# A four-layer graph network on one core: another order of VectorE's round in the second edge layer

## The reference

```python
h = jnp.maximum(_layernorm(x, axis=-1), 0.0)
e = jnp.concatenate([h[src], h[dst]], axis=-1)
e = jax.nn.relu(e @ Wm1 + bm1) @ Wm2 + bm2
e = e * drop_mask                                  # edge_attr_96
m = jax.ops.segment_sum(e, dst, num_segments=n)
z = jnp.concatenate([h, m], axis=-1)
x = x + jax.nn.relu(z @ Wu1 + bu1) @ Wu2 + bu2
```

## Time and profile before

| what | value |
|---|---|
| time, middle of three runs | 6119.12 us (6116.01 to 6123.38) |
| the profiled execution's own time | 6117.6 us |
| its span, from first to last instruction | 6115.7 us |
| busy: PE, DVE, ACT, POOL | 75%, 69%, 57%, 56% of the span |
| the pass `e1` | some 2480 to 3395 us from the span's start |

### The profile page before, as it was taken

The page is one execution under the profiler, slowest core; times in us unless marked ns, Lnnn a source line. Parts: engine busy times, 40 slices in busy tenths (PEclk is TensorE's granted clock), DMA queues, the critical chain, the costliest instruction groups (busy, mean ns, idle before and its releaser), DMA issues. The chain is left out here.

```text
span 6115.7 us, 115642 instructions
## 1 busy us (share of the span) xinstructions
PE 4559.9 (75%) x22351; PEld 2931.6 (48%) x22351; DVE 4229.4 (69%) x13899; ACT 3505.4 (57%) x8824; POOL 3410.0 (56%) x3543
## 2 busy tenths in 40 slices
PE   5776888888799999799999788878888984222222
PEld 1223555555444444466666566656656663222221
DVE  5667888888788888777777688878876663222222
ACT  6996666666699999555555455545545552111110
POOL 0004666666654443344343566566657776777777
PEclk9999999999999999899999787778778885555555
DMA  0002333333344443455555577656657773222222
GB/s 18 0 0 67 101 105 102 104 103 105 98 96 94 94 94 86 105 143 142 141 142 137 150 188 193 181 148 163 163 144 183 184 187 89 61 64 66 63 67 57
DMA packets 1144861, 677.32 MB, mean 111 GB/s; under 512 B 898421, under 2 KB 1096833, under 8 KB 1144744
## 3 DMA queue, kind: packets, MB, share of 16 engines
q1 hardware_dynamic: 1031784, 527.07, 31.7%
q0 software_dynamic: 112960, 148.99, 11.7%
HBM read 445.59 MB, written 232.61 MB: 111 GB/s over the span
## 5 line engine op out<-in xcount | busy, mean ns | idle before, releaser
L724 POOL DMA_INDIRECT xs<-t,idx x1176 | 1110.5, 944 | 951.5 <-DMA idx<-at 573.4
L1197 PE MATMUL bank<-ident,msg 128*96 128x128 f32 (+1 forms) x1568 | 305.5, 329 | 856.5 <-ACT msg L992 771.8
L724 POOL DMA_INDIRECT xs<-c,idx x784 | 763.9, 974 | 291.6 <-issue 233.2
L992 ACT ACTIVATE msg<-xs,now 128x96 f32<-128x96 f32 x784 | 229.3, 364 | 1071.4 <-DMA xs<-c,idx 715.3
L1041 PE MATMUL bank<-cols,before 128*128 128x384 f32 x1756 | 734.0, 520 | 17.3 <-DVE wu_out L1334 14.1
L1495 DVE TENSOR_TENSOR_SCAN aggT<-goes,aggT,bank 96x512 f32<-96x512 f16 (+1 forms) x490 | 620.7, 1267 | 133.9 <-PE bank L1150 115.0
L1197 PEld LDWEIGHTS bank<-ident,msg 128*96 128x96 f32 (+1 forms) x1568 | 218.6, 163 | 1022.7 <-ACT msg L992 650.1
L1208 PE MATMUL bank<-w,aggT 96*128 96x96 f32 (+1 forms) x3136 | 549.9, 334 | 105.2 <-DVE aggT L1495 104.6
L1670 DVE SCALAR_TENSOR_TENSOR y<-bank,now,rows 128x96 f32<-128x96 f32 x392 | 97.2, 310 | 719.1 <-PE bank L1208 719.1
L724 POOL DMA_INDIRECT xd<-in_x_dram,idx x392 | 373.9, 954 | 395.5 <-DVE xn L1565 228.6
L1208 PEld LDWEIGHTS bank<-w,aggT 96*128 96x128 f32 (+1 forms) x3136 | 517.3, 249 | 130.9 <-issue 88.6
(11 more groups left out here) (233 smaller groups left out, 10943.2 us busy)
## 6 DMA issues: line engine op xcount, KB each, us to landing
t<-xn SPq DMA_DIRECT2D x294, 192.0 KB, 2.2
xd<-t SPq DMA_DIRECT2D x294, 192.0 KB, 3.5
goes<-goes_d SPq DMA_DIRECT2D x392, 128.0 KB
xd<-in_x_dram SPq DMA_DIRECT2D x196, 192.0 KB
t<-xo SPq DMA_DIRECT2D x196, 192.0 KB
hd<-t SPq DMA_DIRECT2D x196, 192.0 KB
hs<-t SPq DMA_DIRECT2D x196, 192.0 KB
c<-xn SPq DMA_DIRECT2D x196, 192.0 KB
```

The source lines that it names most:

```text
L724: nc.gpsimd.indirect_dma_start(out=into, out_offset=None, in_=table, in_offset=bass.IndirectOffsetOnAxis(ap=indices, axis=0)).then_inc(don ...
L1197: ins = nc.tensor.transpose(bank[g.at(2)][0:m, c * P:(c + 1) * P], msg[:, g.at(2), c, 0:m], ident[:])
```

## The change

VectorE's list for `e1` is put in another order; no instruction is added or taken away, and no wait is changed.

```diff
                 else:
                     sums = sums_of(ph, lambda g: bank[5][0:D, :], ph["seg"], D, ph["z"])
-                    stages = [(spread, 2), (times_drop, 3), (home_x, 2), (new_x, 5), (edge_moments, 0), (of_round, 0), (sums, 3)]
+                    stages = [(edge_moments, 0), (of_round, 0), (spread, 2), (times_drop, 3), (home_x, 2), (new_x, 5), (sums, 3)]
                 pipelined(dve, EG, stages)
```

## The result

The changed kernel takes 6168.52 us (middle of four runs, 6161.38 to 6173.45), the kernel before 6120.66 (middle of four runs as well): a ratio of 1.0079, 95% interval 1.0063 to 1.0095. It is slower, by 48 us; forecast were 32 us, and a time of 6150 in a range from 6117 to 6172. The profiled execution took 6168.8 us, 51.2 more than the one before.

A forecast was written before the change was run, and what follows sets the result against it. The prediction took PE, waiting on ACT in a 9.02 us ring, to bound the pass; a new VectorE-PE ring of 9.40 us in the loop, 9.29 outside, would add 32 us, giving 6150 us, range 6117 to 6172.

The forecast's parts named there:

- the ring of PE and ACT without VectorE: PE's L1114 waits for ACT's normalizing of `hd`, released by `home_z`; claimed to bind before the change, 9.02 us a round.
- Earlier roots gain nothing: Roots come a round earlier for ACT; claimed no gain, since ACT's normalizing stood idle 0.0 us before `hd`.
- The moments' inputs keep their lead: POOL's gathers ahead of VectorE's moments; claimed the lead shrinks to 23 us and stays, at no cost.
- The new ring: L1150, `sums`, moments, roots, `spread`, `times_drop`, then PE's L1126, L1128, L1150; claimed to bind at 9.40 us in the loop, chance 0.79.
- PE's wait at L1126: PE's `hid` product should wait for `times_drop` in nearly every round, some 0.1 to 0.4 us.
- The sum: All steps from one `sums` to the next: 9.40 us in the loop, 9.29 outside, 875.4 us in 93 rounds.
- last step to `spread`: VectorE's gap from the roots' last operation to `spread`: 0.26 us in the loop, 0.15 in written-out rounds.
- The 0.16 us more between `spread` and `times_drop` in each of 14 turns: Extra VectorE time between these two operations at each turn of the loop, 2.2 us in all.
- the 9.3 to 9.5 that were named as a sign: Round time in us of pass `e1` expected in the changed profile if the forecast held.
- the cover just holds: Rival: `times_drop` still comes in time for L1126, so the time stays at 6119 us; chance 0.13.
- the kernel gets faster: Rival: PE's wait for ACT at L1114 shrinks, by 0.55 us a round at most, down to 6067 us; chance 0.04.
- The clock: Rival: new PE waits make TensorE's clock fall in the pass, giving 6171 to 6290 us; chance 0.04.

The follow-up runs named there:

- e7: Kernel before, with ACT running `home_act` between its two normalizing halves and PE `home_u` between its two transpose halves; 6051.0 us, ratio 0.9897.
- e1: Changed kernel with `sums` put back behind the roots, so only moments and roots work a group further ahead; 6115.2 us, ratio 0.9999 to the kernel before.
- e3: Changed kernel with `times_drop` run before `spread`; 6115.6 us, ratio 1.0001 to the kernel before.
- e5: Changed kernel with one more VectorE operation each round, between the roots and `spread`; 6181.3 us, ratio 1.0107 to the kernel before.
- e6: Changed kernel with one more VectorE operation each round, between `new_x` and `sums`; 6161.5 us, ratio 1.0076 to the kernel before.
- e8: Changed kernel with ACT running `home_act` between its normalizing halves and PE `home_u` between its transpose halves; 6168.3 us, ratio 1.0087 to the kernel before.
- e4: Changed kernel with `spread`'s three waits and turn count moved ahead of the moments; 6138.7 us, ratio 1.0036 to the kernel before.
- e2: Kernel before with `sums` moved in front of moments and roots, which do not work a group further ahead; 6695.0 us, single run.
- e10: Changed kernel with only `spread`'s turn count moved ahead of the moments, its three waits left in place; 6153.2 us, single run.
- e9: Changed kernel with `spread`'s turn count and waits moved ahead of the moments, except the flags' wait; 6151.6 us, single run.

## Why the prediction was right, point by point

- **What bounds the pass before**: the ring of PE and ACT without VectorE. Shown by e7, where cutting it takes 63 us out. It gives more than the 0.55 us a round that PE stood idle, 0.63. Idle time counts from the recorded end of the product before, and in the kernel before four transposes (L1150) are recorded with 0.60 us where the next product starts 0.43 us after them; an idle time of 0.55 can so stand for up to 0.72, which would cover the 0.08. That this is the reason was not tested.
- **Earlier roots gain nothing**: shown by e1. The rule of the Trainium skill that was named there (Perfetto Trace Analysis, "Optimization Strategies": when the matmul engine idles for others, optimize those that block it) agrees with the runs where it is applied to what PE waits for: e7 reorders ACT's list and gains; e1 brings ACT an input that it did not lack, and does not. The row that the prediction read for this, of `hd` in the earlier trace rows, could not show a wait for roots, since ACT waits for them in front of `hs`. The row of `hs` in the kernel before, in the same window, reads 0.0 as well, so the conclusion held:

```profile
L825 ACT ACTIVATE hs<-xs,nmr,rstd 128x96 f32<-128x96 f32 x376 | 143.8, 456 | 0.0
```

- **The moments' inputs keep their lead**: shown by e1. POOL waits longer for `home_x`, 142.0 us in 21 waits (2520 to 3420 us) where it was 3.4 in 11, which the forecast did not say; but VectorE never waits for a gather in that window, so the lead hides it.
- **The new ring and PE's wait at L1126**: shown by e3 (taken off, the loss is gone), e5 against e6 (an operation costs on it and not beside it) and e8 (the other ring does not matter).
- **The sum** was too small by 18.7 us (875.4 forecast, 894.1 measured from `sums` of group 1 to that of group 94). The step that failed is "last step to `spread`": 0.26 us was taken, for one computed address, and the loop's rounds show 0.44. That is 0.18 x 84 = 15 us of the 18.7, and one more comes from the written-out rounds, where 0.15 was taken and the later ones show 0.23. Of the rest, moments and roots took 3.56 us on average where 3.51 was taken, 4.6 us more, and `times_drop` 0.53 where 0.56 was taken, 3.0 us less. The 0.16 us more between `spread` and `times_drop` in each of 14 turns did not come: that pair is 1.20 us apart in every round, where 1.17 was taken, and the two misses cancel by luck. The three waits and the count that stand in front of `spread`, with the register operations that belong to them, were not counted; e4 shows that they make 0.33 of the 0.44. The upper bound of the step, 0.61, held, and so did the range, in which the time lies near the upper end. The round, 9.61 us, lies above the 9.3 to 9.5 that were named as a sign, and near the 9.7 that was to mean a mis-sized term, which it did.
- **The rivals.** That the cover just holds fell with the measured ratio, that the kernel gets faster with it and with e1. The clock did not fall in the changed kernel: 1.00 in the window, with two stalls of PE in each round. It fell in e2, where PE waits 3.15 us in one piece. The rule of the Trainium skill (TensorE: Matmul & The Clock Gate, "A second HAM failure mode: psum-queue depth-cycling"), that short idles between groups of matmuls make the clock swing, does not agree with the changed kernel, whose stalls of 0.30 and 0.55 us left the clock at 1.00. The clock of e2 does fall (0.76 on average), but whether a wait of 3.15 us is what the rule means by a short idle, the section does not say.

## What to carry to other kernels

The first place of a round's list stands behind its last, so a new order of a loop has to be read as a circle: look what each engine's wait used to cover, and sum the ring that closes when the cover is moved. A kernel with several rings runs at the longest, so a reordering of one engine shows nothing until the ring that binds is cut. Between short operations of an in-order engine in a loop, waits, counts and the register operations that come with them have a price of their own; put them where a long operation still runs.

## What the runs showed of the hardware that was not expected

- In VectorE's loop, each wait or count of `spread`, which follows a 0.17 us operation, cost some 0.07 to 0.1 us on average (step 0.44, 0.37, 0.20 and 0.11 us in the changed kernel, e10, e9 and e4). Behind the 1.28 us scan of `sums` it cost nothing (1.20 us from `sums` to the moments with and without it). Part of the price is that of register operations: with the same waits and count the step took 0.23 us without any and 0.40 with two, some 0.09 us each.
- A releaser in the profile can be a coincidence: the same gap in front of `spread` is put down to PE's L1114 in the changed kernel and to "issue" in e8.
- With one wait of about 3.15 us for PE in each round of 15.16 us (e2), the granted clock was 0.76; with two of 0.30 and 0.55 us in a round of 9.6 us (the changed kernel) it was 1.00, and with one of about 1.1 us in a round of 9.6 us (e8, 92.3 us in 86 waits) it was 1.00 too.
